# Band attention rebuilt in the structure of the full attention: loads of operands by groups, paired small products, transposed values, query 0 worked in among the first units

## The reference

```python
# stage 0: 16 heads of 8, band of +-16 keys, token 0 sees and is seen by all
mask = abs(idx[:, None] - idx[None, :]) <= 16
mask = mask.at[0, :].set(True); mask = mask.at[:, 0].set(True)
scores = einsum('bnsd,bntd->bnst', q, k) * 8 ** -0.5
attn = softmax(where(mask, scores, -inf), axis=-1)
out = einsum('bnst,bntd->bnsd', attn, v)
return einsum('bsh,oh->bso', out.transpose(0, 2, 1, 3).reshape(B, S, H), Wo)
```

## Time and profile before

| what | value |
|---|---|
| runs shown | 1253.72, 1248.14, 1250.81 us, median 1250.81 |
| profiled execution | 1252.19 us, its span 1250.5 us |
| TensorE, VectorE, ScalarE, GpSimd busy | 85%, 72%, 59%, 15% of the span |
| mean granted TensorE clock | 0.899 of full |
| projection of the band attention starts | 39.3 us |
| first addition of its result to x | 277.5 us |

### The profile page before, as it was taken

How to read it: one execution, slowest core, us unless ns; L and a number is a source line. 1 busy time by engine, 2 the same in 40 slices (tenths; PEclk the granted TensorE clock), 3 DMA queues, 4 the chain that set the end, 5 groups by cost and what they waited for, 6 DMA issues and landing times.

```text
span 1250.5 us, 32345 instructions
## 1 busy us (share of the span) xinstructions
PE 1065.1 (85%) x12934; PEld 532.7 (43%) x12934; DVE 897.3 (72%) x1221; ACT 741.3 (59%) x1496; POOL 184.7 (15%) x341
## 2 busy tenths in 40 slices
PE   6457887888648799999999998877999999999986
PEld 3135676764214333333334444533333344444443
DVE  4554554556465479999999991364899999999635
ACT  2250222223822339989999994222599899999921
POOL 9500434330008000000000000000000000000000
PEclk9668878779977799999999998678999999999977
DMA  2140212100000523322010100007322300101000
GB/s 82 64 126 23 85 56 85 52 2 1 1 0 0 174 83 67 70 48 49 18 29 18 26 21 20 0 1 227 59 62 52 77 20 20 26 20 27 19 14 34
DMA packets 65913, 58.05 MB, mean 46 GB/s; under 512 B 24944, under 2 KB 50032, under 8 KB 65648
## 3 DMA queue, kind: packets, MB, share of 16 engines
q1 hardware_dynamic: 65776, 56.14, 17.1%
HBM read 29.08 MB, written 26.84 MB: 45 GB/s over the span
## 4 chain that ended last, share of the span: by engine, by line
DVE 39%; PE 27%; issue 17%; POOL 8%; DMA 4%; ACT 3%; SPq 2%; POOLq 0%; DVEq 0%; ACTq 0%
DVE nmf L1355 33%; PE wide L565 16%; PE bank L565 10%; POOL big L535 4%; DMA KQs<-m_dram 3%; ACT xcsq L931 2%; DVE xcsq L1138 1%; DVE nmt L1364 1%; DVE res L1138 1%; SPq L371 1%; ACT big L931 1%; POOL KQs L502 1%; DVE big L1439 1%; DVE x L1138 1%; DMA kq_dram<-big 1%
## 5 line engine op out<-in xcount | busy, mean ns | idle before, releaser
L1355 DVE TENSOR_REDUCE nmf<-wide 128x1 f32<-128x1024 f32 x512 | 586.9, 1201 | 34.7 <-PE wide L565 34.5
L931 ACT ACTIVATE big<-wide 128x512 f32<-128x512 f32 (+2 forms) x773 | 441.9, 601 | 149.3 <-PE wide L565 116.1
L565 PE MATMUL bank<-big,V 128*9 128x128 f32 x8192 | 319.2, 274 | 11.8
L565 PE MATMUL wide<-big,KQs 48*128 48x512 bf16 x1024 | 308.0, 381 | 4.3 <-DVE nmf L1355 3.2
L931 ACT ACTIVATE big<-bank 128x512 f32<-128x512 f32 (+3 forms) x489 | 237.5, 506 | 82.4 <-PE bank L689 61.5
L565 PEld LDWEIGHTS bank<-big,V 128*9 128x9 f32 x8192 | 176.7, 90 | 232.2 <-ACT big L931 222.0
L565 PE MATMUL wide<-KQs,big 50*128 50x512 bf16 x683 | 233.5, 381 | 8.0 <-DMA KQs<-m_dram 6.9
L565 PE MATMUL bank<-KQs,big 50*128 50x512 bf16 x341 | 130.0, 381 | 4.2 <-DMA KQs<-m_dram 3.2
L547 POOL CAST nms<-nmf 128x4 bf16<-128x4 f32 x128 | 23.8, 186 | 715.5 <-DVE nmf L1355 715.5
L1302 DVE TENSOR_REDUCE nm<-wide 95x11 f32<-95x1408 f32 x32 | 51.7, 1620 | 57.5 <-PE wide L565 57.4
L565 PEld LDWEIGHTS wide<-KQs,big 50*128 50x128 bf16 x683 | 52.4, 93 | 83.4 <-ACT big L931 56.0
(11 more groups left out here) (190 smaller groups left out, 1050.6 us busy)
## 6 DMA issues: line engine op xcount, KB each, us to landing
kq_dram<-big SPq DMA_DIRECT2D x48, 256.0 KB, 4.1
o_dram<-big SPq DMA_DIRECT2D x128, 64.0 KB, 1.6
KQs<-k_dram SPq DMA_DIRECT2D x48, 132.0 KB
big<-kq_dram SPq DMA_DIRECT2D x32, 192.0 KB, 4.1
KQs<-kq_dram SPq DMA_DIRECT2D x32, 192.0 KB, 4.6
KQs<-q_dram SPq DMA_DIRECT2D x16, 293.9 KB
m_dram<-nmt SPq DMA_DIRECT2D x128, 8.0 KB
KQs<-m_dram SPq DMA_DIRECT2D x128, 2.0 KB
```

Source lines behind the costliest of these rows:

```text
L565: return nc.tensor.matmul(o, l, r, start=start, stop=stop, **kw)
L931: return nc.scalar.activation(o, i, f, **kw)
L1355: nc.vector.tensor_reduce(nmf[:, (s0 + i) % 4, c:c + 1], wide[:, k:k + 2, :].rearrange("p g c -> p (g c)"), AX.X, ALU.max, negate=True).th ...
```

## The change

The band attention is written again in the form of the full attention. `store_parts`, `load_operands`, `place_shift`, `remainder`, `split_part`, `split_maximum`, `divide`, the hardware loops and the output transposes are gone. In their place:

```diff
-LEAD = 6
+AHEAD_W = 5
+WG = ((0, 4), (4, 4), (8, 3))
...
+        LOADS_W = {2: 4, 6: 5, 10: 6, 14: 7}
...
+            sp.wait_ge(ones_rows, 1)
+            for dram in (kw_dram, kf_dram):
...
+                for b in range(B):
+                    for k in (1, 0):
+                        store(b, k)
+                    if b == 0:
+                        sp.wait_ge(ones_out, 32)
+                        for k in range(2):
+                            sp.wait_ge(partw_out[k], 96)
+                        load_group(0)
+                        load_group(1)
+                for k in range(2):
+                    sp.wait_ge(partw_out[k], 96 * B)
...
+                for u in range(AHEAD_W - 1):
+                    turned(u, mw_dram[u, :, :])
+                    if u:
+                        shift(u - 1)
+                    if u == 1:
+                        load_group(2)
+                load_group(3)
...
+                for u in range(AHEAD_W):
+                    for g, (t, k) in enumerate(WG):
+                        mask_maximum(u, g)
                         for y in range(t, t + k):
+                            maximum(u, g, y)
+                        keep_busy(1, bk(7))
+                    if u == 0:
+                        zero_scores(0)
+                    if u == 2:
+                        zero_scores(1)
+                    if u == 3:
+                        zero_turn()
+                zero_values()
+                for u in range(UNITS):
+                    ahead = u + AHEAD_W < UNITS
+                    if u == 1:
+                        zero_column()
+                    if u % 6 == 3:
+                        pe.wait_ge(pv_evac, u - 1)
+                        keep_busy(12, bk(6 + u % 2))
+                    for g, (t, k) in enumerate(WG):
+                        mask_scores(u, g)
+                        if ahead:
+                            mask_maximum(u + AHEAD_W, g)
                         for y in range(t, t + k):
+                            scores(u, g, y)
+                            if ahead:
+                                maximum(u + AHEAD_W, g, y)
+                        if g == 1 and u:
+                            values(u - 1)
+                values(UNITS - 1)
...
-                        sp.wait_ge(qk_out[n % CBUF], 16 * (n // CBUF))
+                        if b and at == 0:
+                            act.wait_ge(partw_out[int(kind == "q")], 96)
...
-                        pool.wait_ge(x_new, NC * 3)
-                        for r in (32, 96):
-                            pool.memset(kop[r:r + 32, :, :], 1.0).then_inc(ones_rows, 1)
```

More of the change, by code:

```diff
@@ L197, in build @@
         nm_out = [sem(f"nm_out{i}") for i in range(4)]
[L198 removed]
+        nm_in = [sem(f"nm_in{i}") for i in range(8)]
         pv_done, pv_evac = sem("pv_done"), sem("pv_evac")
@@ L429, in full_attention @@
                 for i in range(AHEAD - 1):
-                    turned(i)
+                    turned(s0 + i, m_dram[i, :, :])
                     if i:
@@ L538, in _, with split_shift @@
-            if nst > 0:
-                with pool.Fori(0, UNITS // BODY_W) as i:
-                    for j in range(BODY_W):
-                        pool.wait_ge(exp_done, i * BODY_W + j + 2)
-                        remainder(j % 4, 0, QW)
-            def split_shift(s):
-                pool.wait_ge(mx_read, 4 * (s + 1))
+            def split_shift(s, nm, rows):
+                n = nm.shape[1]
+                first, second = nms[0:rows, s % 4, 0:n], nms[0:rows, s % 4, n:2 * n]
                 if s >= 4:
@@ L748, in windowed_attention, with mask_maximum @@
[L748 to L752 removed]
+                pe.wait_ge(tw, 2)
+                keep_busy(2, bk(6))
+                keep_busy(20, bk(7))
+                def mask_maximum(u, g):
+                    n = len(WG) * u + g
+                    t, k = WG[g]
+                    if g == 0 and u % H % 4 < 2:
+                        pe.wait_ge(opw_in[2 * (4 * (u // H) + u % H // 4) + u % 2], 32)
+                    if n >= 3:
+                        pe.wait_ge(wx_read, n - 2)
+                    mm(bk(g)[0:QT, 0:k * P], identb[0:QT, 0:QT],
+                       maskq[0:QT, t:t + k, :].rearrange("p t k -> p (t k)"))
```

750 lines of the change are left out of this document (343 added, 407 removed).

## The result

The changed kernel takes 1204.7 us (median of 4 runs, 1199.8 to 1210.0), the kernel before 1252.3 in the runs beside it: a ratio of 0.963, 95% interval 0.959 to 0.966. The forecast was 1187 with a range of 1160 to 1226. The direction and the range held, and the gain was 47 us where I had summed 64. The profiled execution took 1205.0 us, span 1203.2.

What follows compares the result with a forecast made beforehand. TensorE was taken to bound the old loop and the new units. First addition to x at 209.6 against 277.5 us, 67.9 less, plus 4 for later stages, gives 1188.3 from 1252.2; less 1.4 for the median, 1187 us, range 1160 to 1226.

Steps and rivals of the forecast that it cites:

- Entry: From the projection at 39.3 us to unit 0 at 98, with the first turned maxima leaving at 81.
- The quotient: Behind unit 0, TensorE waits 2.9 us for query 0's ten small steps, then 0.5 for its column; unit 1 at 104.4.
- A unit in the loop: Band attention's loop: TensorE takes 2.6 us a unit at full clock: masks 1.06, 11 pairs 1.0, values 0.55.
- Clock and late rows: Band attention: 4 us added for late rows at the entry and low clock behind the 3.8 us stop, bounds 0 and 15.
- rival B: Band loop: the old loop's mean clock of 0.81 returns, TensorE's 85 us become about 105; 1212 us, 12% chance.
- Dense products: Band loop: 60 products of 0.214 us each cost TensorE 12.8 us.
- rival D: Slower than before: TensorE at 1.2 GHz from unit 0 to the end, +89 us, 1276 us; 4% chance.
- Output: From the band attention's last values to the first addition to x: 12.2 us, where it was 9 before.
- Later stages: After the first addition to x: 4 us more for the full attentions' 50-row k loads, bounds nothing and 18.
- A: Band loop: small pairs do not pair and cost 0.15 us instead of 0.1, a unit 3.3 us; 1208 us, 15% chance.
- E: Band loop: pairs start together and hide their weights, a unit 2.2 us, entry 4 less; 1172 us, 12% chance.
- C: All three attentions: 50-row loads or SyncE's queue order delay rows, 12 x 1 us and 5 at the entry; 1200 us, 12%.

Runs made afterwards that it cites:

- e1: Changed kernel with each band unit's masks and pairs grouped in two runs, so two switches a unit, not three: 1199.7 us, ratio 0.958.
- e5: Changed kernel with all masks of a band unit together, then all its pairs, in one run: 1206.2 us, ratio 0.964.
- e2: Changed kernel without the 60 dense products in the band attention's loop: 1240.3 us.
- e9: Changed kernel with query 0's column one unit later and without the loop's 60 dense products: 1226.7 us, ratio 0.983.
- e4: Changed kernel with the full attentions' k loads at 48 rows, the rows of ones loaded separately ahead: 1197.6 us, ratio 0.957.
- e8: Changed kernel with a group's four transfers in the full attentions spread over four successive slots: 1194.9 us, ratio 0.958.
- e7: Changed kernel with the band attention's group transfers leaving one a unit, not four together: 1199.9 us, ratio 0.959.
- e11_best_no_dense: Changed kernel with two-run units, query 0's column later, transfers spread in band and full attentions, and no dense products in the loop: 1176.2 us, ratio 0.938.

## Why the prediction was right, and where it missed

Against the profiled execution I had the first addition at 209.6; it came at 227.8, 18.2 late. By my steps:

- **Entry: 2.0 early (unit 0 at 96.0 for 98), in part by luck.** Stores, ScalarE's wait and the turned maxima went as the full attention's rows had said: from the projection's start to the dense products 28.6 us for 27.7, the maxima left at 80.4 for 81. Three other terms were off and nearly cancel. "The projection begins at 39.3 as before" and "GpSimd's lost fills were not what it waited for" were wrong: it began at 35.1, in other profiles at 29, since the window copies ahead of it have less of GpSimd's work beside them, which the last section shows. From the first dense product to the first maxima it was 4.8 us for 8: the rows that I had taken the dense products from, 24 in 8.3 us, were mostly at the low clock (0.63 in their stretch), and here it was full. And from there to unit 0 it was 27.5 us for 23: the leading units take 2.6 us at full clock for 1.85, because their three groups switch as well, and the fifth took 4.6 at 0.50.
- **The quotient: right in kind.** Unit 1 at 102.8 for 104.4, a wait of 3.4 us for 2.9, 0.9 for the column where I had 0.5. The sum has 3.8 for the stop, though its terms, 2.9 and 0.5, make 3.4; it lasted 4.4.
- **A unit in the loop: the term that was mis-sized.** Masks 1.04 (1.06), values 0.61 (0.55), VectorE 2.0 (1.95), ScalarE 1.7 (1.5 to 2.0). "A pair with two loads is near 0.1, I take 1.0": the pairs run at the lower bound, 0.053 each and 0.58 in all, and three changes between full-array and row-tiled products add 0.75, 1.33 together. I had taken a value between two bounds from rows in which no such change occurs: in the kernel before, 125-row products followed the masks without a gap, and 48- and 50-row ones stood only beside their like the earlier trace rows. 26 units, 9.9 us; e1 and e5 show it directly. The last five units were priced too low for the same kind of reason, 2.16 us a unit for 1.6 (1.96 in e1, with one switch less): 3.4 with the last wait.
- **Clock and late rows: the allowance of 4 was too small.** The low clock behind the column cost 5.5 (10.2 us for units 1 and 2 against 6.0, and 3.8 for 2.6 in the dense products), the wait ahead of unit 14 with its own low clock 3.9. The mechanism of rival B in two short pieces, and mean clock still 0.93.
- **Dense products: right in price (2.60 for twelve), wrong in the account.** I booked 12.8 us of pure cost. Without them the kernel is rival D: at 1.2 GHz from unit 1 to the end in the profile, and by their times about so in seven more executions of nine. I had 4% for D with the products in, and held the forms of the work against it. With three switches a unit those forms do not bring the clock back and the products do (e2, e9); with two they do so themselves (e1).
- **Output: 13.3 us for 12.2.**
- **Later stages: 2.4 for 4.** The waits for m_dram rose by 7.5, a part of which e4 gives to the 50 rows; other pieces gave 5 back. This profile is the lowest of eight with the same code, and over all of them it is 2.4 to 6.7 us more than the single profile before, so the 4 is borne out no worse than that.

The loop with its end: 9.9 + 5.5 + 3.9 + 3.4 = 22.7 over; less the allowance of 4 and 1.6 of the early unit 1, and 1.1 for the output: 18.2. Of the rivals A had the nearest number (1208) for a wrong reason, since the pairs are cheaper than I took them and not dearer. E (1172) had the pairs right: they start together and hide their weights, and 2.98 less the three switches is 2.23 us, its 2.2. C (1200) was there in part, as rows that come late behind a group's loads (e8, e7, e4). What the forecast lacks is the switch, which no rival had, and cheap pairs and a low price of the dense products in the entry hid part of it: the number in the range owes something to that.

## What to carry to other kernels

Where small row-tiled products stand among full-array ones, count the changes between the two, not only the columns: group the masks, then the products. Here that also let the clock come back by itself. Spread bulk transfers so that at most one stands ahead of each small row that somebody waits for; here that was worth more than the number of their rows. A wait of a few microseconds on TensorE has to be priced with the clock behind it, and products that seem to be pure cost may be what brings the clock back; take them out in one run before you believe either.

## What the runs showed of the hardware that was not expected

**VectorE's copies beside GpSimd.** The 22 window copies (128x127, float32) took 12.18 us in the kernel before, with GpSimd at its fills and selects throughout:

```profile
26.93 12.18 DVE L1186 COPY big<-xp 128x127 f32<-128x127 f32 x22
```

In the kernel after they take 6.26 us. Two other profiles show what decides. The copies and one of GpSimd's fills, in e11_best_no_dense and then in e7_quarters_band:

```profile
27.71 6.76 DVE L1206 COPY xcsq<-xp 128x127 f32<-128x127 f32 x22
28.33 0.60 POOL L534 MEMSET sel<- 64x512 f32 x1
```

```profile
27.64 3.05 DVE L1206 COPY xcsq<-xp 128x127 f32<-128x127 f32 x22
28.40 2.76 POOL L533 MEMSET sel<- 64x512 f32 x1
```

In e11 the fill slips in between two copies, and from there on a copy that meets one of GpSimd's instructions ends when that one ends, up to 2.0 us later. In e7 the copies begin 0.07 us earlier and follow each other without a break, 0.14 us each, and it is the fill that lasts until the last copy has ended. So the two engines hold each other up here, one whole instruction at a time, and which one pays hangs on a few hundredths of a microsecond. Fills that nobody waits for were not free. No run changed GpSimd's work alone, so that the 12.18 us of before come from it rests on the traces.

**Two courses of the same entry.** The first 30 us of identical code end 4 to 6 us apart from one kernel's profile to another's, 0.4% of the time; a single profile can hide or feign a gain of that size. The copies take 6.3 to 6.8 us in the six profiles with the late entry and 3.1 in the seven with the early one, so 3.2 to 3.7 us of it are theirs. Whether one kernel takes both courses no run shows, since each has one profile.

**A clock that never came back.** 150 us of TensorE busy without a gap, at 0.50 throughout (e2_no_dense); and the same products with one switch a unit less, in which the clock came back within 7 us (e1_two_runs).
